# A state-space kernel: eleven of 48 states scaled by C after a transposition, in ScalarE's copies

## What is computed

```
def step(h, inp):
    ul, dl, bl, cl = inp
    dA = jnp.exp(dl[..., None] * A)
    h = dA * h + (dl * ul)[..., None] * bl[:, :, None, :]
    y = jnp.einsum('bkdn,bkn->bkd', h, cl)
    return (h, y)
...
y = y0 + y1 + y2 + y3 + y4 + y5 + y6 + y7
```

## Time and profile before

| what | us |
|---|---|
| median of 3 runs | 15,633.26 |
| span of the profiled execution | 15,638.3 |
| VectorE busy | 14,604.3 (93%) |
| GpSimd busy | 13,820.4 (88%) |
| TensorE busy (products) | 12,948.2 (83%) |
| ScalarE busy | 8,897.0 (57%) |
| DMA traffic, mean | 158 GB/s |

### The profile page before, as it was taken

How to read it: one execution, slowest core, us unless ns; L and a number is a source line. 1 busy time by engine, 2 the same in 40 slices (tenths; PEclk the granted TensorE clock), 3 DMA queues, 4 the chain that set the end, 5 groups by cost and what they waited for, 6 DMA issues and landing times.

```text
span 15638.3 us, 128313 instructions
## 1 busy us (share of the span) xinstructions
PE 12948.2 (83%) x42560; PEld 7615.4 (49%) x42560; DVE 14604.3 (93%) x8593; ACT 8897.0 (57%) x8571; POOL 13820.4 (88%) x5892
## 2 busy tenths in 40 slices
PE   7887888878888788887888878888788887888878
PEld 4553355533555335553355533555335553355533
DVE  8998989989899899998999989999899998999988
ACT  4455745457454674556744567445674456744567
POOL 7997979979799798997989978899788997889978
PEclk8999999999999999999999999999999999999999
DMA  5662256622566225662256622566225662256622
GB/s 180 211 214 104 86 180 213 211 101 86 185 212 211 100 84 187 214 210 98 82 193 212 210 95 81 193 213 213 93 78 199 213 211 92 76 200 213 211 87 77
DMA packets 696921, 2473.06 MB, mean 158 GB/s; under 512 B 79292, under 2 KB 101064, under 8 KB 696264
## 3 DMA queue, kind: packets, MB, share of 16 engines
q1 hardware_dynamic: 696264, 2464.85, 45.9%
HBM read 2448.81 MB, written 15.73 MB: 158 GB/s over the span
## 4 chain that ended last, share of the span: by engine, by line
POOL 47%; issue 18%; DVE 13%; PE 11%; DMA 7%; ACT 3%; DVEq 0%; POOLq 0%; SPq 0%; ACTq 0%
POOL room L1043 24%; POOL room L1086 7%; DMA room<-bc_rows 7%; POOL room L1052 5%; POOL room L1078 4%; POOL room L1089 4%; DVE room L1279 4%; DVE room L1212 3%; PE bank L621 3%; POOL room L1033 3%; DVE room L1220 3%; PE bank L556 2%; PE bank L407 2%; DVE u L1169 1%; DVE room L1299 1%
## 5 line engine op out<-in xcount | busy, mean ns | idle before, releaser
L1043 POOL TENSOR_TENSOR room<-room 128x1024 f32<-128x1024 f32 x3072 | 7161.8, 2369 | 0.6
L1212 DVE TENSOR_TENSOR_SCAN room<-bank,room 128x1024 f32<-128x1024 f32 x3072 | 6936.5, 2278 | 75.7 <-POOL room L1043 71.7
L556 PE MATMUL bank<-room,identity 128*128 128x256 f32 x24576 | 5985.2, 389 | 188.5 <-DVE room L1220 188.5
L556 PEld LDWEIGHTS bank<-room,identity 128*128 128x128 f32 x24576 | 4758.9, 195 | 1333.5 <-DVE room L1220 269.6
L825 ACT ACTIVATE bank<-room,a 128x1024 f32<-128x1024 f32 x3072 | 3411.3, 1115 | 3273.9 <-DVE room L1212 3258.4
L621 PE MATMUL bank<-room,identity 128*128 128x512 f32 x6144 | 3011.5, 641 | 860.8 <-DVE room L1299 728.4
L1279 DVE TENSOR_TENSOR_SCAN room<-bank,room 128x1024 f32<-128x1024 f32 x1536 | 3431.5, 2274 | 54.1 <-POOL room L1086 33.6
L1220 DVE TENSOR_TENSOR room<-room,bank 128x1024 f32<-128x1024 f32 x2304 | 2764.1, 1200 | 387.3 <-PE bank L526 374.1
L621 PEld LDWEIGHTS bank<-room,identity 128*128 128x128 f32 x6144 | 1204.8, 204 | 2667.3 <-issue 1257.2
L1086 POOL TENSOR_TENSOR room<-room 128x1024 f32<-128x1024 f32 x768 | 2224.3, 2919 | 56.2 <-ACT room L908 26.7
L1052 POOL TENSOR_TENSOR room<-room 128x1024 f32<-128x1024 f32 x768 | 1817.1, 2366 | 344.1 <-DVE room L1212 343.0
(11 more groups left out here) (115 smaller groups left out, 8767.1 us busy)
## 6 DMA issues: line engine op xcount, KB each, us to landing
room<-bc_rows SPq DMA_DIRECT2D x4608, 512.0 KB, 4.4
wx<-in_w_x SPq DMA_DIRECT2D x65, 162.0 KB
bc_rows<-xdbl SPq DMA_DIRECT2D x72, 128.0 KB, 5.3
pictures<-in_x SPq DMA_DIRECT2D x8, 768.0 KB, 10.9
out_x<-pictures SPq DMA_DIRECT2D x8, 768.0 KB, 7.2
win<-in_w_in SPq DMA_DIRECT2D x16, 288.0 KB, 6.1
room<-in_w_in SPq DMA_DIRECT2D x16, 288.0 KB, 5.0
room<-in_w_out SPq DMA_DIRECT2D x16, 288.0 KB, 5.6
```

Source lines behind the costliest of these rows:

```text
L556: ins = nc.tensor.matmul(dst[line][part], identity[:, :], src[line][part], start=(i == 0 and n == 0 and line == 0), stop=(n == N - 1 and l ...
L1043: nc.gpsimd.tensor_tensor(source0[:, g % SOURCES, :], du0[:, j, :], b_ring0[:, g % BROWS, :], ALU.mult).then_inc(S["source"], note("source ...
L1212: nc.vector.tensor_tensor_scan(run(state0[:, g % STATES, :]), run(whole(DECAY0[g % 2])), run(source0[:, g % SOURCES, :]), 0.0, ALU.mult, A ...
```

## The change

In layer 0 the units are divided among three instead of two. Of the 48 units of a scan, 10 (n = 2, 6, 10, and 12 for j = 0) are weighed by GpSimd, 27 by VectorE and 11 are **turned** (n = 4, 8, 14 for j = 0; n = 4, 8, 12, 14 for the others). A turned unit has no weighing on VectorE and no spread of C:

- TensorE turns the state in eight transpositions of 128 x 128 into WORK (`turn_state`), so that pixels lie on the partitions.
- There C is one number per partition: ScalarE scales by it while it copies the eight pieces out of PSUM into one of two SBUF buffers (`scale_state`), in its step two units on.
- TensorE turns the eight pieces back straight into the sums (`sum_turned`), two units on (`TURN_LAG`). Every second line is mirrored by a permutation in place of the identity (`turning`).

C is itself turned once per scan (`turn_c`, a new piece "c" at j = 1, n = 10) and kept by ScalarE (`keep_c`). Since a turned piece holds whole lines, the sums of the column scans stay in the order of the scan, and `collect` and `begin_sums` bring them into picture order and back. The pieces move to GpSimd's new units. The softplus of a pass moves from unit 14, two passes ahead, to unit 1, one pass ahead. Two weight buffers share one tensor to make room.

```diff
-    return n in (2, 5, 8, 11)
+    return n in ((2, 6, 10, 12) if j == 0 else (2, 6, 10))
+def by_turn(i, j, n):
+    return n in ((4, 8, 14) if j == 0 else (4, 8, 12, 14))
+def by_vector(i, j, n):
+    return not by_pool(i, j, n) and not by_turn(i, j, n)
...
-    if n == (5 if j == 1 else 2) and ahead < PASSES:
+    if n == (6 if j == 1 else 2) and ahead < PASSES:
...
+    if i < K - 1 and (j, n) == (1, 10):
+        return "c", i + 1
...
+            def turn_state(b, g):
+                wait_free(0, 1)
+                pe.wait_ge(S["scan"], at("scan", UNITS[g], b))
+                for k in range(CHUNKS):
+                    ins = nc.tensor.matmul(whole(WORK[0])[:, k * P:(k + 1) * P],
+                                           state0[:, g % STATES, k * P:(k + 1) * P], identity[:, :],
+                                           start=True, stop=True, is_transpose=True)
+                ins.then_inc(S["turned"], note("turned", UNITS[g]))
+                free[0] = free[1] = ("scaled", UNITS[g], b)
...
+            def sum_turned(b, g):
...
+                pe.wait_ge(S["scaled"], at("scaled", UNITS[g], b))
...
+                for k in range(CHUNKS):
+                    part = state_turned[:, s, k * P:(k + 1) * P]
+                    ins = nc.tensor.matmul(whole(YACC)[:, k * P:(k + 1) * P], part, turn,
+                                           start=(i == 0 and n == 0 and k % 4 == 0), stop=(n == N - 1),
+                                           is_transpose=True)
...
                     if g < len(UNITS) and by_vector(*UNITS[g]):
                         spread_c(b, *UNITS[g])
+                    if g < len(UNITS) and by_turn(*UNITS[g]):
+                        turn_state(b, g)
                     if g >= SUM_LAG and by_pool(*UNITS[g - SUM_LAG]):
                         sum_states(b, g - SUM_LAG)
...
+                    if g >= TURN_LAG and by_turn(*UNITS[g - TURN_LAG]):
+                        sum_turned(b, g - TURN_LAG)
...
+            def scale_state(b, g):
...
+                act.wait_ge(S["turned"], at("turned", (i, j, n), b))
+                for k in range(CHUNKS):
+                    cut = slice(k * P, (k + 1) * P)
+                    ins = nc.scalar.activation(state_turned[:, t % TURNS, cut], whole(WORK[0])[:, cut],
+                                               ACT.Identity, scale=c_turned[:, i % 2, k, n:n + 1])
...
+                    if 0 <= g - 2 < len(UNITS) and by_turn(*UNITS[g - 2]):
+                        scale_state(b, g - 2)
```

More of the change, by code:

```diff
@@ L74, in piece @@
         return "xd", i + 1, QUARTERS.index((j, n))
-    if i < K - 1 and j == 2 and n in (8, 11):
-        return "rest", i + 1, int(n == 11)
+    if i < K - 1 and j == 2 and n in (6, 10):
+        return "rest", i + 1, int(n == 10)
+    if i < K - 1 and (j, n) == (1, 10):
+        return "c", i + 1
     if i == K - 1 and (j, n) in GATES:
@@ L96, in stored, with columns @@
     return v[:, 0, :, :], v[:, 1, :, :]
+def columns(ap):
+    return ap.rearrange("p (r c) -> p c r", c=SIDE)
 def lines_in(order, h, of, line):
@@ L543, in begin_sums @@
                     for h in range(2):
-                        nc.tensor.matmul(bank[:, YACC + h, :], identity[:, :], y[:, j, halves(h)],
-                                         start=True, stop=False)
+                        before = y[:, j, halves(h)]
+                        if SCANS[i][1] == "cols":
+                            before = columns(y[:, j, :])[:, h * (SIDE // 2):(h + 1) * (SIDE // 2), :]
+                        nc.tensor.matmul(bank[:, YACC + h, :], identity[:, :], before, start=True, stop=False)
             def sum_states(b, g):
@@ L550, in sum_states @@
                 pe.wait_ge(S[kind], at(kind, (i, j, n), b))
-                src, dst = stored(state0[:, g % STATES, :]), lines(whole(YACC), SCANS[i][1])
+                order = "mirror" if SCANS[i][1] == "mirror" else "rows"
+                src, dst = stored(state0[:, g % STATES, :]), lines(whole(YACC), order)
                 for h in range(2):
                     for line in range(2):
-                        part = lines_in(SCANS[i][1], h, 2, line)
+                        part = lines_in(order, h, 2, line)
                         ins = nc.tensor.matmul(dst[line][part], identity[:, :], src[line][part],
@@ L566, in scans0 @@
                     last = g - 1
-                    if 0 <= last < len(UNITS) and not by_pool(*UNITS[last]):
+                    if 0 <= last < len(UNITS) and by_vector(*UNITS[last]):
                         pe.wait_ge(S["weigh"], at("weigh", UNITS[last], b))
@@ L588, in scans0 @@
                         sum_states(b, g - 2)
-                    if 0 <= last and n not in (1, 2) and not put_off(g) and not by_pool(*UNITS[last]):
+                    if g >= TURN_LAG and by_turn(*UNITS[g - TURN_LAG]):
+                        sum_turned(b, g - TURN_LAG)
+                    if 0 <= last and n not in (1, 2) and not put_off(g) and by_vector(*UNITS[last]):
                         sum_states(b, last)
@@ L830, in collect @@
                 act.wait_ge(S["sum"], at("sum", (i, j, N - 1), b))
-                nc.scalar.activation(y[:, j, :], whole(YACC), ACT.Copy).then_inc(S["ysum"], note("ysum", (i, j)))
+                dst, src = y[:, j, :], whole(YACC)
+                if SCANS[i][1] == "cols":
+                    dst, src = columns(dst), src.rearrange("p (c r) -> p c r", c=SIDE)
+                nc.scalar.activation(dst, src, ACT.Copy).then_inc(S["ysum"], note("ysum", (i, j)))
             def scans0(b):
@@ L1232, in scans0 @@
                         i, j, n = UNITS[g]
-                    if g > 0 and not by_pool(*UNITS[g - 1]):
+                    if g > 0 and by_vector(*UNITS[g - 1]):
                         weigh(b, g - 1)
```

68 lines of the change are left out of this document (54 added, 14 removed).

## The result

The changed kernel takes 16,924.28 us, the median of four runs (16,910.80 to 16,966.16), beside 15,638.28 us for four runs of the kernel before on the same chip: **slower, a ratio of 1.083, 95% interval 1.0815 to 1.0845**. The forecast was 16,360 us, with a range up to 17,080.

The account below looks back on a forecast made before the run. VectorE's work plus waits for TensorE was taken as the bound. 134.9 + 20.2 + 4.85 + 1.6 = 161.5 us a scan, 11.3 more than 150.2, times 64 is 723 us: 16,360 us, range 15,400 to 17,080.

Parts of the forecast that it names:

- VectorE's own work: VectorE in one scan: weighing 27 units, not 36, cuts its bare work from 144.9 to 134.9 us.
- units behind a turned unit (5, 9, 13): Transposition, scaling and spread take 4.7 us against 4.29: 0.4 us of wait in 8 of 11 turned units, 3.2 us.
- start of the steps: two dt steps' old wait, collect: Pass starts: the dt steps' low-clock waits stay, and the collect waits up to 1.0 us for a later sum.
- unit 7 of the middle step: dt in the queue, and the clock: dt projection at unit 6 of j = 1, with sums queued ahead of the spread: 6.9 us, 2.6 us over.
- the other units 7, 11 and 15: the queue: Sums queue ahead of the spread: x projections 4.4 us, turning C 1.7, remainders 3.0, unit 14 4.25.
- the same units: new falls of the clock: TensorE's idle time about turned units: one new fall to the low clock taken per scan, 1.6 us.
- The prices: Eight transpositions on TensorE taken at 0.87 us, 0.11 each; eight scaling copies on ScalarE at 2.4 us.
- the rule about full rows: TensorE: most steps with products of full rows keep their clock, so one new fall was taken, 1.6 us.
- The case that it named and priced for eight falls: Every turned unit's stretch falls to the low clock: 172.7 us a scan, 17,080 us; up to eight falls within 0.62.
- The slowest rival: Transpositions count as idleness, TensorE stays at the low clock throughout: 232 us a scan, 20,900 us; chance 0.04.
- What would show it: Signs: VectorE's spread wait rises from 5.3 to some 26 us a scan; GpSimd and VectorE under 90%; loads 0.11 us apart.

Follow-up runs that it names:

- the run with fillers: The changed kernel plus four zero-weight products behind the spread that follows each turned unit, 11 x 4 a scan: 16,379.69 us, ratio 1.0465.
- the probe: The changed kernel with 200 transpositions, 100 ordinary f32 products and 200 transpositions ahead of TensorE's first work: one run, 17,024.64 us.
- the last kernel: The changed kernel with turned sums earlier, pooled sums later, column order kept between column scans, zero-weight products and first units' sums spread out: 15,375.69 us, ratio 0.9839.

## Why the prediction was right in its direction, and what it got too small

The direction, the mechanism and the range held; the time came out 564 us (3.4%) above the forecast. Term by term for one scan; the forecast's column regroups its terms (3.25 of the 4.85 us of the dt steps and the collect's 1.0 make 4.25; 2.6 and the other 1.6 make 4.2; 4.4, 1.7, 3.0 and 4.25 make 13.35). The waits measured are VectorE's at each unit, as means over scans 2 to 7 of images 2 to 8 (42 scans):

| term, us a scan | forecast | measured |
|---|---|---|
| VectorE's own work | 134.9 | 137.1 |
| units behind a turned unit (5, 9, 13) | 3.2 | 0.2 |
| start of the steps: two dt steps' old wait, collect | 4.25 | 5.7 |
| unit 7 of the middle step: dt in the queue, and the clock | 4.2 | 5.1 |
| the other units 7, 11 and 15: the queue | 13.35 | 12.9 |
| the same units: new falls of the clock | 1.6 | 9.6 |
| sum | 161.5 | 170.6 |

The measured scans themselves take 170.8 us on the mean. Without the clock's 8.0 us the errors of the other terms (2.2, -3.0, 1.45, 0.9 and -0.45 us) come to 1.1 us; that they nearly cancel is in part luck.

- *The queue.* At the full clock the units wait 2.15, 0.79, 1.44, 1.54 and 1.66 us where the prediction has 2.2, 0.85, 1.7, 1.5 and 1.7. Those behind the 12.9 are the ones of the 42 scans in which no low stretch fell into the wait (a single one for the 1.44), and the run with fillers shows four of the five in one scan.
- *The prices.* Eight transpositions take 1.04 to 1.06 us with the tail, 0.11 each, as taken from the weight loads; eight scalings 2.17 us, where 2.4 was taken. With that the 0.4 us behind each turned unit vanished: 3.2 us too many.
- *VectorE's work.* It fell by 9.0 us (146.06 to 137.05), not 10.0. The 144.9 us that the prediction starts from are those of the short stretch: 1.1 of the 2.2 us in the table come from that, and since its 150.2 us lack the same weighing, the forecast of the time does not change. Nine weighings went; an instruction that has waited no longer overlaps the one before it (0.06 to 0.08 us on the mean), and some ten weighings wait where five did. That is less than half of the missing 1.0 us; the rest is open.
- *The step that failed* is the clock's: "I take one, near the low end, as most steps with products of full rows keep their clock: 1.6 us". A scan has 6.2 low stretches where it had 1.8. The prediction saw the idle time about the turned units and set the number by the products in the crowded step. Both count. Over the 42 scans a low stretch stood between the weighing before and the late one at the two units behind an x projection (128 rows) in 25 of 84 cases, behind the turning of C in 41 of 42, behind remainders in 66 of 84 and at the three units 15 in 46 of 126 (behind dt, whose fall was foreseen, in 42 of 42). That is 4.2 new falls a scan where one was taken, at 2.3 us each where 1.6 was taken. With the fillers it was 0, 5, 0 and 0 (dt: 16). So the rule about full rows held for most x projections, but not for the others, and without the idle time ahead of them few steps fall. The case that it named and priced for eight falls, 172.7 us a scan, is nearer to the 170.8 measured than the forecast is. Its 1.6 us for each was also low: in the scan shown a fall cost 1.7 us (3.81 against 2.15) to 3.3 us (4.82 against 1.54).
- *The slowest rival* is refuted by the probe. The Trainium skill, TensorE: Matmul & The Clock Gate, Part 4: PE-mode transpose, says that work in transpose mode does not count as activity; here f32 transpositions alone went from 0.21 to 0.11 us apart, the granted clock stayed at 1.00 through the rest of two blocks of two hundred, and the measurement decides. The same page's section "A second HAM failure mode: psum-queue depth-cycling" says that short idle times between groups of products can make the clock swing; the fillers agree, with 546 low stretches becoming 277.
- *What would show it* named units 7, 11 and 15, a wait of some 26 us and both engines under 90%: the places and the shares came true (VectorE 137.05 of 166.41 us, 82%; GpSimd 86%), the wait was 35.0 us.

What stays open: which share of a fall belongs to which gap, and which to the piece behind it. The fillers show that without the gaps most falls go; no run took away one gap alone or changed a piece alone. That the column scans' waits come from the strided copy was tried only together with the move of unit 0's sum, not by itself. No filler was tried on the kernel before, whose dt steps make VectorE wait 3.4 us a scan on the mean of the same 42 scans (some 217 us in all); so it is not shown how much of the last kernel's 254 us the new division itself brings.

## What to carry to other kernels

When work moves to another engine, write down for the engine that feeds the bound what its queue holds between two deadlines, and then how long it stands idle ahead of that and what piece comes next: here the queue was foreseen to half a microsecond a scan, and the falls of the clock behind idle time cost 9.6 us beside it. The offload could be made to pay, by 1.6%: 1,549 us of 16,924 went with another order of the same work, a contiguous copy and some filler. Two small rules did it here: put a ready product into each gap while another engine copies, and put what a third engine waits for (the transpositions) ahead of sums that nobody waits for.

## What the runs showed of the hardware that was not expected

- An f32 transposition of 128 x 128 on TensorE goes at 0.11 us, half of an ordinary f32 product of that shape. Transpositions alone brought the clock up (0.21 us apart at first, then 0.11) and held it at 1.00.
- Behind idle times of 0.6 to 1.5 us, several in a row with 0.6 to 2.8 us of products between, the granted clock fell to 0.50, though no single one was long: nearly always where dt or the turning of C came next (83 of 84 cases), less often at an x projection (25 of 84). 44 products of zero weights a scan removed half of the falls and made the kernel 545 us faster.
- ScalarE's copy of 128 x 1024 f32 from PSUM into a column order takes 1.88 to 1.97 us, into a contiguous one 1.00 to 1.02.
